# A Mamba, window-attention, convolution and memory block in one kernel: head tables made by PE and ScalarE, and a new order of the prepared work

## What is computed

```
xn   = layernorm(x);  xp = xn @ w_xproj          # dt_in (64), B (64), C (64)
delta= softplus(dt_in @ w_dt + b_dt)             # 512 x 128
h    = exp(delta*A) * h + (delta*xn) * B         # scan over 512 tokens, 128 channels x 64 states
y    = sum over states of h * C
q, k, v = x @ wq, x @ wk, x @ wv                 # 16 query heads, 4 key/value heads of 8
ao   = softmax(q k^T / sqrt(8) + bias) v         # windows: blocks of 32 queries see 96 keys
conv = silu(4-tap causal convolution of x + b)
eo   = softmax(x dec^T / sqrt(128)) dec          # 512 memory slots
out1 = x + .2*ao@wo + .45*(y + x*D)@w_ssm_out + .15*conv + .2*(x@w_wm + .3*eo)
out  = out1 + layernorm(out1) @ (int4(W) + a@b) + bias
```

## Time and profile before

| | |
|---|---|
| median of three runs | 1186.4 us |
| profiled execution | 1190.31 us |
| its span, first to last instruction | 1188.4 us |
| VectorE busy | 1060.7 us (89%) |
| PE busy | 892.2 us (75%), granted clock 0.863 |
| ScalarE, GpSimd busy | 816.3 us, 816.2 us |
| batch, steady | about 141.5 us, VectorE busy 132 us of it |
| DMA | 155.39 MB, mean 131 GB/s |

### The profile page before, as it was taken

One profiled execution on the slowest core, in us unless ns is written; L12 is line 12 of the kernel. 1 busy time (PEld: TensorE's weight loads), 2 busy tenths in 40 slices (PEclk: granted clock), 3 DMA queues, 4 the chain that ended last, 5 costly groups with the idle time before them and its releaser, 6 DMA issues. The chain is left out here.

```text
span 1188.4 us, 19151 instructions
## 1 busy us (share of the span) xinstructions
PE 892.2 (75%) x4292; PEld 365.1 (31%) x4292; DVE 1060.7 (89%) x2434; ACT 816.3 (69%) x2199; POOL 816.2 (69%) x558
## 2 busy tenths in 40 slices
PE   4457877777787777877778778778779777786875
PEld 1122233323333232332333223323333323322332
DVE  3569899988999899898999979998999979999993
ACT  4357885778748777577857778487875868656772
POOL 7547676766767667676767767686776767767673
PEclk9557888888888899888988989888898879899898
DMA  4744355544463555626545445564546254463530
GB/s 114 138 128 142 100 142 151 147 116 127 136 174 102 133 136 130 168 74 160 148 138 156 119 130 130 125 173 99 158 128 176 77 159 128 131 171 103 148 107 9
DMA packets 124133, 155.39 MB, mean 131 GB/s; under 512 B 32722, under 2 KB 57062, under 8 KB 124006
## 3 DMA queue, kind: packets, MB, share of 16 engines
q1 hardware_dynamic: 123110, 153.47, 47.9%
q0 software_dynamic: 512, 0.27, 0.2%
q10 hardware_dynamic: 384, 0.26, 0.1%
HBM read 137.63 MB, written 4.52 MB: 120 GB/s over the span
## 5 line engine op out<-in xcount | busy, mean ns | idle before, releaser
L1347 POOL TENSOR_TENSOR prod<-hst,C 128x1024 f32<-128x1024 f32 x256 | 604.1, 2360 | 307.7 <-DVE hst L1159 307.6
L1159 DVE TENSOR_TENSOR_SCAN hst<-decay,bank 128x512 f32<-128x512 f32 x512 | 617.8, 1208 | 0.2 <-DVE bank L1153 0.2
L634 ACT ACTIVATE decay<-wide,A_rep 128x512 f32<-128x512 f32 x512 | 362.6, 715 | 144.3 <-DVE hst L1159 91.6
L1153 DVE TENSOR_TENSOR bank<-bank,B 128x512 f32<-128x512 f32 x512 | 348.3, 680 | 52.5 <-PE bank L879 25.7
L879 PE MATMUL bank<-spread,sel_bc 96*128 96x512 bf16 x512 | 218.8, 429 | 186.1 <-DVE hst L1159 170.2
L648 ACT ACTIVATE prob<-s_sb,nmax 128x96 f32<-128x96 f32 x512 | 184.7, 362 | 1.0 <-DVE nmax L1172 0.5
L879 PEld LDWEIGHTS bank<-spread,sel_bc 96*128 96x128 bf16 x512 | 53.7, 105 | 374.9 <-DVE hst L1159 317.9
L901 PE MATMUL bank<-prod,sel_red 128*32 128x512 f32 x1024 | 164.4, 720 | 0.4 <-POOL prod L1347 0.4
L911 PE MATMUL bank<-k,q 128*128 128x384 f32 x256 | 117.8, 543 | 12.9 <-DVE nmax L1172 12.8
L1352 POOL TENSOR_TENSOR prob<-prob,pinv 128x384 f32<-128x384 f32 x128 | 108.2, 846 | 19.6 <-DVE pinv L1180 15.2
L657 ACT ACTIVATE probT<-bank 96x512 f32<-96x512 f32 x128 | 75.0, 586 | 58.5 <-PE bank L918 58.1
(11 more groups left out here) (180 smaller groups left out, 928.9 us busy)
## 6 DMA issues: line engine op xcount, KB each, us to landing
wide<-dt_rows SPq DMA_DIRECT2D x512, 256.0 KB, 4.4
vw<-v_tok SPq DMA_DIRECT2D x80, 64.0 KB, 3.5
spread<-parts SPq DMA_DIRECT2D x88, 32.0 KB, 3.6
x_sb<-in_L_attn_x_dram SPq DMA_DIRECT2D x8, 256.0 KB, 4.8
dt_rows<-sp_t SPq DMA_DIRECT2D x8, 256.0 KB, 4.3
out_dram<-outb SPq DMA_DIRECT2D x8, 256.0 KB, 2.3
q<-qn SPq DMA_DIRECT2D x112, 16.0 KB
vw<-v_tok SPq DMA_DIRECT2D x16, 48.0 KB, 3.4
```

Source lines behind the costliest of these rows:

```text
L634: nc.scalar.activation(decay[:, q, :], wide[m % SLOTS][:, s % 2, :], ACT.Exp, scale=A_rep[:, g:g + 1]).then_inc(exp_done, 1)
L1153: v.tensor_tensor(uP[s % 4][:, :], uP[s % 4][:, :], B2[p][:, :], ALU.mult).then_inc(dbx_done, 1)
L1159: v.tensor_tensor_scan(hst[:, s % 4, :], decay[:, s % 4, :], uP[s % 4][:, :], 0.0, ALU.mult, ALU.add).then_inc(scan_done, 1)
L1347: g.tensor_tensor(prod[:, 2 * (m % 4):2 * (m % 4) + 2, :], hst[:, 2 * (m % 2):2 * (m % 2) + 2, :], C2[p][:, :].unsqueeze(1).to_broadcast([ ...
```

## The change

- Softplus and its inputs move ahead: xaT 14, xnT 16, dti 18, dtpre 20, softplus exp and the +1 in unit 21, logarithm 23, rounding 24. B and C move to units 31 and 32, the memory's es0 from 31 to 27 with its maximum two units behind (before: one), pt0 to 33, q, k, v to 58, 60, 62. The attention blocks start three units earlier.
- SyncE's store of the output stands at pair 14 and the store of the delta rows at pair 15 (before: 10 and 18).
- The 32 placing DMAs of a batch are gone. PE computes q as before, and ScalarE makes four copies of it, each with a per-partition mask (`q_mask`) as its scale; k is computed with weights repeated to 128 columns (`wk_rep`), and copied in four pieces of 32 partitions; both read the job in two halves, one unit apart. v is 16 products, one for each block of 96 tokens, copied at once.
- The convolution's gate reads `jobP` on VectorE with its bias; the missing summand is a second product in `project`.
- The text of the change speaks of "all u*B on VectorE"; no line of u*B is in the diff.

```diff
-JOB_AT = {12: ("t", "back"), 14: ("p", "xaT"), 15: ("p", "xnT"), 22: ("t", "zT"), 25: ("t", "ffn"), ...
+JOB_AT = {12: ("t", "back"), 14: ("p", "xaT"), 16: ("p", "xnT"), 18: ("p", "dti"), 20: ("p", "dtpre"), ...
-    ... "softplus_exp": 28, "sum": 31, "softplus_logs": 30, "rounding": 32, "log1p": 31, ...
+    ... "softplus_exp": 21, "sum": 21, "softplus_logs": 23, "rounding": 24, "log1p": 25, ...
-    "y_start": 5, "tanh": 37, "gate": 39,
+    "y_start": 5, "tanh": 38, "gate": 39,
-ROWS_AT = {"store": 10, "rows": 18}
+ROWS_AT = {"store": 14, "rows": 15}
-SCORES_AT = {3 + 33 * k // 10: k for k in range(NBLK)}
+SCORES_AT = {33 * k // 10: k for k in range(NBLK)}
...
+            def query_copies(half, job):
+                for r in (2 * half, 2 * half + 1):
+                    ins = nc.scalar.activation(q4[:, :, r, :], job[:, :].rearrange("p (n q) -> p n q", q=W), ACT.Copy,
+                                               scale=q_mask[:, r:r + 1])
+                return ins
+            def key_copies(half, job):
+                for g in (2 * half, 2 * half + 1):
+                    ins = nc.scalar.activation(k4[32 * g:32 * g + 32, g, HALO:HALO + L], job[32 * g:32 * g + 32, :],
+                                               ACT.Copy)
+                return ins
...
-                    ins = mm(job[0:KVH * HD, :], wk_s[:, :], xaT[p][:, HALO:HALO + L], start=True, stop=True)
+                    ins = mm(job[:, :], wk_rep[:, :], xaT[p][:, HALO:HALO + L], start=True, stop=True)
                 elif name == "v":
-                    for t in range(NT):
-                        ins = mm(job[:, t * 32:(t + 1) * 32], xaT[p][:, HALO + t * 128:HALO + (t + 1) * 128],
-                                 wv_s[:, :], start=True, stop=True)
+                    for n in range(NBLK):
+                        ins = mm(job[0:3 * W, n * 32:(n + 1) * 32], xaT[p][:, n * W:n * W + 3 * W], wv_s[:, :],
+                                 start=True, stop=True)
...
+                    mm(jobP[:, :], cs_id[:, :], cv_v[:, :], start=False, stop=False)
                     ins = mm(jobP[:, :], cs_id[:, :], cs[:, :], start=False, stop=False)
...
-                v.scalar_tensor_tensor(cs[:, :], cv_a[:, :], 1.0, cv_v[:, :], ALU.add, ALU.mult).then_inc(cv_step, 1)
+                v.scalar_tensor_tensor(cs[:, :], jobP[:, :], bconv_col, cv_a[:, :], ALU.add, ALU.mult).then_inc(cv_step, 1)
+                wait(dve, cv_step, B * N_CV + CV["cs"])
+                dve.sem_inc(done["m"], 1)
```

More of the change, by code:

```diff
@@ L39 @@
 PRE = {n: i for i, n in enumerate(["xaT", "xnT", "dti", "dtpre", "B", "C", "q", "k", "v"])}
-MEM = {n: i for i, n in enumerate(["es0", "conv", "es1", "pt0", "es2", "pt1", "es3", "pt2", "pt3"])}
+MEM = {n: i for i, n in enumerate(["es0", "pt0", "conv", "es1", "es2", "pt1", "es3", "pt2", "pt3"])}
 TAIL = {n: i for i, n in enumerate(["proj", "back", "zT", "ffn"])}
 N_PRE, N_MEM, N_TAIL = len(PRE), len(MEM), len(TAIL)
-JOB_AT = {12: ("t", "back"), 14: ("p", "xaT"), 15: ("p", "xnT"), 22: ("t", "zT"), 25: ("t", "ffn"),
[4 rows of a table removed]
+JOB_AT = {12: ("t", "back"), 14: ("p", "xaT"), 16: ("p", "xnT"), 18: ("p", "dti"), 20: ("p", "dtpre"),
[3 rows of a table added]
 EMPTY_LAG = 0
@@ L313, in hybrid_block_kernel @@
         N_FIRST_DMA, N_W_DMA = 13, 18
[L315 to L330, removed]
         def xin(B):
@@ L454, in load_weights @@
                 assert n == N_W_DMA
[L456 to L472, removed]
             def front(B, p):
@@ L558, in scale_xn, with second_half @@
                 ins.then_inc(ln_step, 1)
+            def query_copies(half, job):
[8 more added lines that the diff above has]
+                return ins
+            def second_half(name, B):
+                copies = query_copies if name == "q" else key_copies
+                copies(1, jobP).then_inc(done["p"], 1)
             def pre_job(name, B, p, front=False):
@@ L562, in pre_job @@
                 wait_job(act, "p", B, name)
+                if name in "qk" and not front:
+                    (query_copies if name == "q" else key_copies)(0, job)
+                    return
                 if name == "xaT":
@@ L577, in pre_job @@
                 elif name == "k":
-                    ins = nc.scalar.activation(kn, job[0:KVH * HD, :], ACT.Copy)
+                    for half in range(2):
+                        ins = key_copies(half, job)
                 elif name == "v":
-                    wait(act, v_in, B * 16 * N_V_DMA)
-                    ins = nc.scalar.activation(v_tok[:, :, :, 0:HD].rearrange("p t g h -> p (t g) h"),
-                                               job[:, 0:128].rearrange("p (a h) -> p a h", h=HD), ACT.Copy)
-                else:
-                    if not first(B):
-                        wait_heads(act, B - 1)
-                    ins = nc.scalar.activation(qn[:, :], job[:, :], ACT.Copy, scale=-float(HD) ** -0.5)
+                    ins = nc.scalar.activation(vw[:, :, :, :].rearrange("p n g h -> p (n g h)"), job[0:3 * W, :], ACT.Copy)
+                else:
+                    for half in range(2):
+                        ins = query_copies(half, job)
                 ins.then_inc(done["p"], 1)
@@ L691, in conv_bias @@
                 wait_job(act, "m", B, "conv")
+                wait(act, ready["t"], B * N_TAIL - N_TAIL + 1)
                 nc.scalar.activation(cv_v[:, :], jobP[:, :], ACT.Identity, bias=bconv_col).then_inc(cv_step, 1)
[L693 to L694 removed]
+                wait(act, cv_step, B * N_CV + CV["v"])
             def conv_tanh(B):
@@ L753, in body @@
                         empty_job(*JOB_AT[s - EMPTY_LAG], B, p)
+                    fam, name = JOB_AT.get(s - 1, ("", ""))
+                    if fam == "p" and name in "qk" and not last(B):
+                        second_half(name, B + 1)
                     if s == AT["tanh"]:
```

65 lines of the change are left out of this document (28 added, 37 removed), and 7 rows, old and new, of the table JOB_AT.

## The result

The changed kernel takes 1203.03 us (median of 4 runs, 1200.67 to 1206.90) against 1186.04 us (1185.50 to 1186.75) for the kernel before on the same chip: ratio 1.0146, 95% interval 1.0119 to 1.0173. It is slower, by 1.5%; 1170 had been forecast. The profiled execution took 1206.9 us with a span of 1205.1, which is 16.7 more than the span before.

A forecast was written before the change was run, and what follows sets the result against it. VectorE was taken to bound the kernel, busy 1060.7 of 1188.4 us, so only its idle time could be won. Terms -44 + 12 + 19 + 1.5 + 2 - 7 = -16.5 took 1186.4 to 1170 us; range 1148 to 1196.

The forecast's parts named there:

- the end of a batch becomes the bound: Rival, chance 0.22: values in PE's queue ahead of u, plus late scores, make the kernel slower, 1193 or 1199 us.
- Together +19: Batch boundaries, values on PE and late first scores: +3.0 us at four plain ones, +2.4 at three back edges; bounds 0 to +42.
- When v starts: End of a batch: PE may start the values 9.5 us after unit 58 starts, behind ScalarE's copies of q and k.
- How long v takes: Values on PE, 32 passes with 96 weight columns: 6.2 us at the slow clock, 3.7 fast, 7.7 at most.
- When u of unit 1 is wanted: Next batch's unit 1: VectorE wants u at 12.8 us from unit 58's start, ready at 16.4, a wait of 3.6.
- What follows v: Start of a batch: reduction, u, projection and scores queue behind the values; first scores 1.3 to 3.2 us late, 1.5 taken.
- At the back edges: Three loop jumps: VectorE's own 2.8 us hides the values, scores come 2.9 late; 5.6 for 3.2, +2.4 each.
- The middle, -44: Mid-batch: moved store, early softplus and es0 at 27 remove VectorE's waits for the memory's maximum, u and scores, -44 us.
- Unit 21, +12: Softplus' exp and +1 share unit 21: VectorE waits 1.9 us for ScalarE in six batches, +12 us.
- Set-up, -7: Before the first scan: the values' twelve issues no longer hold back wide loads; -7 us, between -9 and -4.
- the first batch, +2,: Start of the kernel: ScalarE's copies of q, k and v stand ahead of its issue of the parts; +2 us, 0 to +3.
- The gate, +1.5,: Convolution's gate on VectorE: same length from PSUM, added wait for its own end 0.2 us, +1.5 in all.

The follow-up runs named there:

- run 5: Changed kernel with the values' products in the transposed probabilities' bank, in three pieces over units 61, 62 and 63: 1161.51 us, ratio 0.9788.
- Run 1: Kernel before with only SyncE's store of the output moved from pair 10 to 14: 1151.59 us, ratio 0.9713.
- run 3: Changed kernel with the store of the output put back from pair 14 to pair 10: 1199.52 us, ratio 1.0108.
- Runs 7 to 11: Softplus steps or zT in other units: run 7 on the changed kernel, 1203.50 us; four kernels built on run 5, 1166.46, 1160.55, 1167.48 and 1159.04 us.
- run 2: Kernel before with the store at pair 14 and VectorE's rounding of the softplus in unit 33 instead of 32: 1152.83 us, ratio 0.9713.
- run 7: Changed kernel with softplus' +1 on VectorE in unit 22 instead of 21: 1203.50 us, ratio 1.0144.
- run 6: Changed kernel with the values' products issued once more, unused, into the attention's bank ahead of the wait for the keys: 1204.93 us, ratio 1.0156.

## Why the prediction was wrong

**The direction.** Of the cases, "the end of a batch becomes the bound" came true, with 0.22; even its worst figure, 1199, lies 4 us below the measured 1203. The step that failed is the price of the boundaries, "Together +19", in the parts on v on PE and on the start of a batch. It measures +34 in the trace: v starts 2.3 us later than forecast, what follows v costs 2.4 for 1.5, and the three boundaries where v was to be hidden cost 8.3 on average for 5.6. Taking v out of the way (run 5) gives back 41 us, waits for the output and for other scores among them. The point from which it decides was 5.1 us more a boundary; 34 / 7 = 4.9 nearly reached it, and the other terms did the rest.

Its parts:
- *When v starts:* forecast 9.5 us behind the start of unit 58, measured 11.8 (11.4 to 11.8 at the four plain boundaries). This is where the first wait was missed. VectorE starts unit 58 of batch 1 at 316.37; its u*B at 328.04 is that of the next batch's unit 0. From the reading of pt3 on, the chain of q and k took nearly what I had added up, but pt3 was read at 3.1 and not at 1.1. PE had been slow in the units before:

```profile
311.49 1.94 PE L876 MATMUL bank<-prod,sel_red 128*32 128x512 f32 x8
...
314.24 1.88 PE L922 MATMUL bank<-mdiag,mprob 128*128 128x128 f32 x8
...
316.37 0.70 DVE L1136 TENSOR_TENSOR bank<-bank,B 128x512 f32<-128x512 f32 x1 [0.23 <-PE bank L852]
```

```profile
306.00:311.00 5.00, 1.16 (x11) 0.36 (x11) 5.00 (x8) 3.90 (x15) 3.15 (x3) 0.81 0.66 173
311.00:316.00 5.00, 5.00 (x22) 2.81 (x23) 5.00 (x8) 1.24 (x2) 4.59 (x3) 0.51 0.34 111
```

  The kernel before has q in unit 52 and k in unit 54. There, units 52 to 54 (312 to 317 us) have a granted clock of 1.00, and the same pt2 product takes 1.15 us:

```profile
315.05 1.15 PE L948 MATMUL bank<-mdiag,mprob 128*128 128x128 f32 x8 [0.32 <-ACT qn L586]
```

  With q and k moved to 58 and 60, PE was busy 1.16 of 5.00 us before the fall to 0.51. The prediction gave the slow clock to v alone. No run puts q and k back, so that their move is what brings it about is my reading; that v came 2.3 us late is measured.
- *How long v takes:* forecast 6.2 at the slow clock, measured 5.33 at 0.50. Near, on the safe side. It is far from the 3.5 that follows, as an estimate, from the Trainium skill, "TensorE: Matmul & The Clock Gate", section "LDWEIGHTS (loading the stationary operand)", as the slow row had said; run 5's 3.13 at 1.00 is near it.
- *When u of unit 1 is wanted:* forecast 12.8, measured 13.1 (VectorE was ready at 333.93 - 4.45 = 329.48). Right. So the wait is 4.45 for 3.6: v 2.3 later, v and u 1.1 shorter, the deadline 0.3 later.
- *What follows v:* also wrong: forecast 1.3 late with the fast clock, 3.2 slow, 1.5 taken. The reduction and u behind v are slow too (1.94 and 0.61), and the wait is 2.3 to 2.4. I had given v the slow clock and what follows it the fast one; the 3.2 was the nearer end.
- *At the back edges:* forecast +2.4 each on the ground that VectorE's own jump hides v. They cost 7.4 to 8.9 us where 5.6 was forecast: the jump (2.20) is followed by the waits for u and scores (2.05 and 4.04) and doesn't hide them. At batch 7, where VectorE has no jump, the wait for u alone is 5.1.

**The middle, -44.** The size was right: in the changed kernel the maximum has no wait at all. The reason was half right. Run 1 shows that moving the store is enough, run 3 that in the new order of jobs it isn't needed. I had put both edits in one term and named the first as cause.

**Unit 21, +12.** It measures 16.7 us, 15.7 of them in the six batches that were meant. ScalarE's work was priced rightly (1.63 + 0.62 behind the decay; the terms as listed add up to 242.9 and not 243.1), its start was late: dtpre's readers wait 0.75 us for PE before it. Runs 7 to 11 show that this term is hard to get rid of: other places for the chain made the time between 6 us longer and 2.5 us shorter, by the medians.

**Set-up, -7** (6.9 measured) and **u*B, 0** were right, **the first batch, +2,** near (first u*B at 45.69 for 44.63, other waits bring it to some 3.5). **The gate, +1.5,** comes to 4.7 if its wait for its own end, some 0.2 us a batch, is taken as forecast: 0.3 to 0.8 us of waiting for ScalarE's tanh in seven batches (3.2 in all) were not seen. Nor has it the same length from PSUM: 0.75 us for 0.67. **Not seen at all:** 3.9 us at the output in two batches, 4.2 us of waits for scores away from the boundaries, and 1.6 in the tail.

The sum: 15 for the boundaries, 4.7 for unit 21, 3.2 for the gate, 3.9 + 4.2 + 1.6 for what was not seen, 1.5 for the first batch: 34 us, for 1203 - 1170 = 33. That the two agree to 1 us is in part luck, since waits under 0.4 us were not followed one by one.

## What to carry to other kernels

A job that moves from DMAs to PE (TensorE) is not priced by its busy time (40.1 us for all the values here) but by what stands behind it in PE's queue: the same products in another free bank, cut in three between the large ones, turned a loss of 17 us into a gain of 25. Give the slow clock to everything that follows in a stretch and not only to its first product. Look also at the place that a job leaves: in the units from which q and k had gone PE idled, its clock fell, and the chain that v waits for began 2 us late. Of a change of many tables, try the lines one at a time: one number (the store, from pair 10 to 14) gave 1151.6 us, the lowest median of all.

## What the runs showed of the hardware

- VectorE's operation on two SBUF operands that starts 0.49 us behind GpSimd's product takes 2.41 us (run 1) for 0.69 (run 2). If it comes first, the product pays: 2.79 us for 2.35 in run 5, where the rounding starts 0.12 us before it:

```profile
238.36 0.69 DVE L1132 SCALAR_TENSOR_TENSOR sp_t<-sp_t,xn 128x512 f32<-128x512 f32 x1
238.48 2.79 POOL L1346 TENSOR_TENSOR prod<-hst,C 128x1024 f32<-128x1024 f32 x1 [0.34 <-DVE hst L1160]
```

- A one-operand +1 on VectorE is caught too: up to 2.49 us for 0.43 (run 7).
- The granted clock left 1.00 (2.4 GHz) for a mean of 0.70 in a stretch in which PE's records fill 3.84 of 3.90 us, behind 3.00 us filled with the same small products at 1.00 (run 6). 32 fp32 passes of 32 columns with 96 weight columns took 2.83 us (run 6) and, in three pieces, 3.13 (run 5) at 1.00, and 5.33 at 0.50 (the changed kernel); the reduction's eight passes 1.07 and 1.94.
